# A fused attention and feed-forward layer on one core: even parts of the relative values, the output mask at the end of the step, and a low part on GpSimd

## The reference

```python
xn  = layernorm(x)
q,k,v = projections of xn with biases                     # [B,H,S,8]
idx = clip(r[None,:] - r[:,None], -128, 128) + 128
scores = (einsum('bhqd,bhkd->bhqk', q, k) + einsum('bhqd,qkd->bhqk', q, rel_k[idx])) / sqrt(8)
w   = softmax(scores)
att = einsum('bhqk,bhkd->bhqd', w, v) + einsum('bhqk,qkd->bhqd', w, rel_v[idx])
ffn = relu(xn @ ternary(W1).T + b1) @ ternary(W2).T + b2
out = x + att @ Wo.T + bo + ffn
```

## Time and profile before

| | us |
|---|---|
| median of 3 runs | 612.52 (611.48 to 612.66) |
| the profiled execution | 610.89 |
| its span in the profile | 609.1 |
| busy in the span: PE, DVE, ACT, POOL | 533.7, 508.8, 466.0, 149.5 |
| end of the first stage (barrier on SP's queue) | 108.8 |
| transposes of step 0, of step 127 | 112.6, 567.4 |
| table work of DVE in the second chunk (L563 to L581) | 42.5 to 45.5 |

### The profile page before, as it was taken

The page is one execution under the profiler, slowest core; times in us unless marked ns, Lnnn a source line. Parts: engine busy times, 40 slices in busy tenths (PEclk is TensorE's granted clock), DMA queues, the critical chain, the costliest instruction groups (busy, mean ns, idle before and its releaser), DMA issues.

```text
span 609.1 us, 25643 instructions
## 1 busy us (share of the span) xinstructions
PE 533.7 (88%) x10578; PEld 489.7 (80%) x10578; DVE 508.8 (84%) x1353; ACT 466.0 (77%) x993; POOL 149.5 (25%) x170
## 2 busy tenths in 40 slices
PE   0777796689999999999999999999999999999996
PEld 0354464578989898898989898999898989898896
DVE  6798967699888989888888888888888888989734
ACT  1686885589887978898889788878887898879511
POOL 4345554032222213131313131313122222210000
PEclk9997999799999999999999999989999999999778
DMA  8312565911000010101010101010100001000243
GB/s 184 125 45 77 129 111 133 161 27 29 12 20 15 17 23 8 27 7 28 4 29 4 30 3 30 2 30 5 26 11 22 13 19 18 15 3 4 64 116 104
DMA packets 75835, 26.34 MB, mean 43 GB/s; under 512 B 55008, under 2 KB 72904, under 8 KB 75592
## 3 DMA queue, kind: packets, MB, share of 16 engines
q1 hardware_dynamic: 74832, 24.19, 17.9%
q10 hardware_dynamic: 888, 0.53, 0.3%
HBM read 13.16 MB, written 8.40 MB: 35 GB/s over the span
## 4 chain that ended last, share of the span: by engine, by line
PE 51%; DVE 15%; issue 14%; ACT 1%; DVEq 0%; ACTq 0%
PE ps_r L878 11%; PE ps_r L880 10%; PE ps_s L950 8%; PE ps_o L848 6%; DVE obd L1143 5%; PE ps_t L938 5%; PE ps_o L852 4%; PE ps_o L850 4%; DVE mcol L1180 3%; DVE big L1113 2%; DVE mx L1109 2%; PE ps_s L902 1%; PE ps_y L862 1%; PE ps_t L927 1%; PE ps_o L927 1%
## 5 line engine op out<-in xcount | busy, mean ns | idle before, releaser
L756 POOL COPY by_q_room<-qrel 96x256 uint32<-96x256 uint32 x120 | 98.3, 821 | 340.8 <-PE ps_t L938 293.9
L1113 DVE TENSOR_TENSOR big<-p,big 128x512 f16<-128x512 f32 x256 | 172.1, 673 | 0.1
L1027 ACT ACTIVATE big<-p 128x512 f16<-128x512 f32 x256 | 161.5, 632 | 6.1 <-PE ps_r L880 6.1
L878 PE MATMUL ps_r<-gwin,big 128*128 128x17 f16 x1024 | 133.3, 207 | 0.0
L880 PE MATMUL ps_r<-gwin,big 128*128 128x9 f16 x1024 | 132.6, 203 | 0.0
L1180 DVE TENSOR_REDUCE mcol<-ps_t 128x4 bf16<-128x512 bf16 x128 | 88.2, 689 | 53.0 <-PE ps_t L938 53.0
L880 PEld LDWEIGHTS ps_r<-gwin,big 128*128 128x128 f16 x1024 | 128.2, 164 | 0.0
L878 PEld LDWEIGHTS ps_r<-gwin,big 128*128 128x128 f16 x1024 | 125.9, 162 | 0.0
L1007 ACT ACTIVATE p<-ps_s 128x512 f32<-128x512 f32 x128 | 77.8, 607 | 46.0 <-PE ps_s L950 44.0
L848 PE MATMUL ps_o<-v_sb,big 128*128 128x33 f16 x1024 | 90.6, 178 | 21.5 <-DVE obd L1143 7.8
L848 PEld LDWEIGHTS ps_o<-v_sb,big 128*128 128x128 f16 x1024 | 80.9, 96 | 33.0 <-issue 31.7
(11 more groups left out here) (110 smaller groups left out, 873.7 us busy)
## 6 DMA issues: line engine op xcount, KB each, us to landing
kst<-big SPq DMA_DIRECT2D x48, 64.0 KB, 2.0
qrel<-qr_dram SPq DMA_DIRECT2D x192, 16.0 KB
qbd<-q_dram SPq DMA_DIRECT2D x192, 16.0 KB
q_dram<-by_q_room SPq DMA_DIRECT2D x8, 256.0 KB, 3.1
y_dram<-big SPq DMA_DIRECT2D x4, 512.0 KB, 4.4
qr_dram<-big SPq DMA_DIRECT2D x4, 512.0 KB, 8.3
big<-y_dram SPq DMA_DIRECT2D x4, 512.0 KB, 6.9
out<-big SPq DMA_DIRECT2D x4, 512.0 KB, 3.2
```

The lines of the kernel that those rows point to most:

```text
L878: nc.tensor.matmul(r_ps[:, q % QH, :], hi, win, start=(q % QH == 0 and kh == 0), stop=False, skip_group_check=True)
L1027: nc.scalar.activation(probs[:, k // 8, 0, kh, k % 8, :], p32[:, k % 2, kh, :], ACT.Copy).then_inc((hi0_ready, hi_ready)[kh], 1)
L1113: nc.vector.tensor_tensor(probs[:, k // 8, 1, kh, k % 8, :], p32[:, k % 2, kh, :], probs[:, k // 8, 0, kh, k % 8, :], ALU.subtract).then_i ...
```

## The change

Seven edits. In the main stage: (1) `REL_PARTS` is eight parts of 4 queries, from step 9 + 8 bg on, so every step has one; the sums follow (at 13 + 8 bg + 4 half). (2) The mask of the outputs moves from the start of the next step to the end of its own, after the head mask. (3) The low part of the second 128 keys is made on POOL, with a semaphore of its own. (4) POOL's half copies are dealt to other steps (`HALVES`), at most two in a step, the last in step 1 of the group itself. In the first stage: (5) `residues` moves from ACT to POOL, between its other work; (6) the low parts of hidden blocks 2 and 3 move from POOL to DVE, ahead of the copies of V; (7) the clearing of `qbd` moves ahead of the first deviations.

```diff
-REL_PARTS = (4, 4, 4, 4, 5, 5, 6)
+REL_PARTS = (4,) * 8
...
# first stage, ACT
-                wait(act, hlo_ready, c * FT + f - 1)
+                wait(act, hlo_ready[1 - f // 2], FT // 2 * (c + f // 2 - 1) + f % 2 + 1)
...
-                    residues(q_hi, 0, i, p).then_inc(qhi_ready, 1)
...
-                    residues(q_lo, 1, i, p).then_inc(qlo_ready, 1)
# first stage, POOL
+            def residues(part, s, i, p):
+                pool.wait_ge((nat_hi_ready, nat_lo_ready)[s], 2 * i + p + 1)
+                own = part.rearrange("p (n j x q y) -> p n j x q y", n=NQB, j=J, x=B // 2, y=2)[:, :, :, 2 * i + p, :, :]
+                for b in range(2):
+                    ins = nc.gpsimd.tensor_copy(own[:, :, :, :, b],
+                                                q_nat[:, i % 2, s, :, 2 * p + b, :].rearrange("p n (q j) -> p n j q", j=J))
...
+            nc.gpsimd.memset(v["qbd"]...).then_inc(zero_q, 1)
             inverse_deviation(0, 0)
             inverse_deviation(1, 1)
-            nc.gpsimd.memset(v["qbd"]...).then_inc(zero_q, 1)
...
                     if not last:
                         inverse_deviation(2 * i + p + 2, p)
-                    for f in range(FT):
-                        hidden_low(2 * i + p, f)
+                    residues(q_hi, 0, i, p).then_inc(qhi_ready, 1)
+                    hidden_low(2 * i + p, 0)
+                    residues(q_lo, 1, i, p).then_inc(qlo_ready, 1)
+                    hidden_low(2 * i + p, 1)
# first stage, DVE, after normalize and before the copies of V
+                    for f in range(FT // 2, FT):
+                        dve.wait_ge(hhi_ready, c * FT + f + 1)
+                        nc.vector.tensor_tensor(hid[:, 1, f, :], hf[:, f % 2, :], hid[:, 0, f, :],
+                                                ALU.subtract).then_inc(hlo_ready[1], 1)
# main stage, POOL
-    BY_Q = ((), (), (), (0,), (1,), (2,), (), (3,))
+    HALVES = (((2, 1), (3, 0)), ((3, 1),), (), (), ((0, 0),), ((0, 1),), ((1, 0), (1, 1)), ((2, 0),))
...
+            def low_part(qb, k):
+                pool.wait_ge(hi_ready, UNITS * qb + k + 1)
+                nc.gpsimd.tensor_tensor(probs[:, k // 8, 1, 1, k % 8, :], p32[:, k % 2, 1, :],
+                                        probs[:, k // 8, 0, 1, k % 8, :], ALU.subtract).then_inc(lo1_ready, 1)
...
+                    su = qb * BG + k // 8 + (k % 8 >= 4)
+                    for x, half in HALVES[k % 8] if 0 < su < NQB * BG else ():
                         pool.wait_ge(qrel_in, (su + 1) * (16 * NDMA))
                         pool.wait_ge(scores_ready, 8 * (su - 1) + 2 * x + 2)
                         pool.wait_ge(maxT_ready, n + 1)
-                        half_pair(x, 0)
-                        pool.wait_ge(half_copied, n + 2)
-                        pool.wait_ge(scores_ready, n + 2)
-                        half_pair(x, 1)
+                        half_pair(x, half)
+                    if unit(qb, k - 1):
+                        if n + 1 < ALL:
+                            pool.wait_ge(half_copied, n + 2)
+                            pool.wait_ge(scores_ready, n + 2)
+                        low_part(*unit(qb, k - 1))
# main stage, PE
-                pe.wait_ge(lo_ready, KH * (n + 1))
+                pe.wait_ge(lo0_ready, n + 1)
+                pe.wait_ge(lo1_ready, n + 1)
...
+                if first == 0:
+                    pe.wait_ge(lo0_ready, UNITS * qb + 8 * bg + 8)
+                    pe.wait_ge(lo1_ready, UNITS * qb + 8 * bg + 8)
...
-                        part = k + UNITS * back - (10 + 8 * bg)
+                        part = k + UNITS * back - (9 + 8 * bg)
# main stage, DVE
-                    if unit(qb, k - 4):
-                        mask_outputs(*unit(qb, k - 4))
...
-                        low_part(*unit(qb, k - 1), 0)
+                        low_part(*unit(qb, k - 1))
...
-                    if unit(qb, k - 1):
-                        low_part(*unit(qb, k - 1), 1)
...
+                    if unit(qb, k - 3):
+                        mask_outputs(*unit(qb, k - 3))
```

More of the change, by code:

```diff
@@ L381, in hidden @@
                                      bias=bcol[:, 2 + f:3 + f]).then_inc(hhi_ready, 1)
[L383 to L389, removed]
             copy_xT(0, 0)
@@ L401, in body @@
                         act.wait_ge(nat_out[i % 2], 32)
+                        act.wait_ge(qhi_ready, 2 * i - 2)
+                        act.wait_ge(qlo_ready, 2 * i - 2)
                     nc.scalar.activation(q_nat[:, i % 2, 0, :, 2 * p:2 * p + 2, :], natural(ps_o[:, :]),
                                          ACT.Identity, bias=bcol[:, 0:1]).then_inc(nat_hi_ready, 1)
-                    act.wait_ge(nat_hi_ready, c + 1)
-                    residues(q_hi, 0, i, p).then_inc(qhi_ready, 1)
                     if not (last and p == 1):
@@ L431, in inverse_deviation @@
                 nc.gpsimd.tensor_tensor(rstd[:, p, :], vare[:, p, :], neghalf[:, :], ALU.pow).then_inc(rstd_ready, 1)
+            def residues(part, s, i, p):
[4 more added lines that the diff above has]
+                                                q_nat[:, i % 2, s, :, 2 * p + b, :].rearrange("p n (q j) -> p n j q", j=J))
+                return ins
             def hidden_low(c, f):
                 pool.wait_ge(hhi_ready, c * FT + f + 1)
-                nc.gpsimd.tensor_tensor(hid[:, 1, f, :], hf[:, f % 2, :], hid[:, 0, f, :], ALU.subtract).then_inc(hlo_ready, 1)
+                nc.gpsimd.tensor_tensor(hid[:, 1, f, :], hf[:, f % 2, :], hid[:, 0, f, :], ALU.subtract).then_inc(hlo_ready[0], 1)
+            nc.gpsimd.memset(v["qbd"][:, :, :, :, :].rearrange("p s g h c -> p (s g h c)").bitcast(F32), 0.0).then_inc(zero_q, 1)
             inverse_deviation(0, 0)
             inverse_deviation(1, 1)
-            nc.gpsimd.memset(v["qbd"][:, :, :, :, :].rearrange("p s g h c -> p (s g h c)").bitcast(F32), 0.0).then_inc(zero_q, 1)
             def body(i, last):
@@ L630, in down @@
                 for f in range(FT):
-                    pe.wait_ge(hlo_ready, c * FT + f + 1)
+                    pe.wait_ge(hlo_ready[f // 2], FT // 2 * c + f % 2 + 1)
                     for t in range(CH):
@@ L721, in build_main @@
         shifted0, shifted, exp0_ready, hi0_ready = sem("shifted0"), sem("shifted"), sem("exp0_ready"), sem("hi0_ready")
-        hi_ready, lo_ready = sem("hi_ready"), sem("lo_ready")
+        hi_ready, lo0_ready, lo1_ready = sem("hi_ready"), sem("lo0_ready"), sem("lo1_ready")
         rsum_ready, gwin_ready, ewin_ready = sem("rsum_ready"), sem("gwin_ready"), sem("ewin_ready")
@@ L760, in body @@
                     n = UNITS * qb + k
-                    for x in BY_Q[k % 8] if not (last and k >= 8) else ():
-                        su = qb * BG + k // 8 + 1
+                    su = qb * BG + k // 8 + (k % 8 >= 4)
+                    for x, half in HALVES[k % 8] if 0 < su < NQB * BG else ():
                         pool.wait_ge(qrel_in, (su + 1) * (16 * NDMA))
@@ L1004, in exponentials @@
                 act.wait_ge(shifted0, n + 1)
-                wait(act, lo_ready, KH * (n - 1))
+                wait(act, lo0_ready, n - 1)
                 nc.scalar.activation(p32[:, k % 2, 0, :], ps_s[:, k % 2, 0, :], ACT.Exp, scale=SCALE).then_inc(exp0_ready, 1)
                 act.wait_ge(shifted, n + 1)
+                wait(act, lo1_ready, n - 1)
                 nc.scalar.activation(p32[:, k % 2, 1, :], ps_s[:, k % 2, 1, :], ACT.Exp, scale=SCALE).then_inc(exp_ready, 1)
@@ L1109, in maximum, with low_part @@
                 nc.vector.tensor_tensor(mx[:, :], s0[:, :], ps_s[:, k % 2, 1, :], ALU.max).then_inc(max_ready, 1)
[L1111 to L1114, removed]
+            def low_part(qb, k):
+                dve.wait_ge(hi0_ready, UNITS * qb + k + 1)
+                nc.vector.tensor_tensor(probs[:, k // 8, 1, 0, k % 8, :], p32[:, k % 2, 0, :],
+                                        probs[:, k // 8, 0, 0, k % 8, :], ALU.subtract).then_inc(lo0_ready, 1)
             def low_outputs(qb, k):
@@ L1168, in relative_of @@
                     for half in range(2):
-                        at = 14 + 8 * bg + 3 * half
+                        at = 13 + 8 * bg + 4 * half
                         if k == at % UNITS and (at < UNITS or unit(qb, -1)):
@@ L1244, in _ @@
             outputs(UNITS - 3)
-            low_part(NQB - 1, UNITS - 1, 0)
-            low_part(NQB - 1, UNITS - 1, 1)
+            low_part(NQB - 1, UNITS - 1)
             low_outputs(NQB - 1, UNITS - 3)
```

5 lines of the change are left out of this document (2 added, 3 removed).

## The result

The changed kernel takes 565.12 us (564.79 to 565.31, four runs) against 612.12 (611.48 to 612.66, four runs beside it): ratio 0.9232, 95% interval 0.9216 to 0.9248, 47 us less. The forecast was 573.5 with a range of 560 to 597. The direction and the place of the gain were right.

The account below looks back on a forecast made before the run. Neither PE nor DVE alone bounds it: pv hangs on transposes, reduce and mask. Span 609.1 + 5 (first stage) - 1.3 (early steps) - 42.7 (117 steps) = 570.1, so 573.5 us for the median; range 560 to 597.

Parts of the forecast that it names:

- The chain through the mask: Main loop: pv hangs on transposes, reduce, mask; the mask at the step's end saves 0.29 us per step.
- The term for the uneven steps: Main loop: eight parts of 4 queries remove PE's 0.49 us wait for the maximum in one step of eight.
- DVE's margin: Main loop: the maximum ends 0.7 us before its transposes, 0.3 with sums; the mask ends as the next reduce is due.
- The port: Main loop: POOL and DVE instructions with SBUF operands exclude each other; head mask waits for POOL's low part, ending at 3.4.
- Rival S: Each step: POOL and DVE exclude each other for every instruction; 4.33 us a step, 124 over the forecast, 697; chance 0.07.
- a pushed L1113: Main loop: a POOL copy delays DVE's low part by 0.15, up to 0.8 in two steps of eight; nothing set.
- the low part's leaving: Main loop: the second low part goes from DVE to POOL, taking 0.58 us a step off DVE.
- The ten early steps: Ten steps before relative products: DVE loses some seven low parts and PE's waits before pv go; 1.3 us saved.
- The first stage: Projections and feed-forward: clearing qbd earlier -3.4, loop through POOL +7.7, last chunks +2.4, gap at the end -2.0; +5.
- the price of a copy: First stage: a POOL copy of 256 f16 elements taken at 0.61 us, making a chunk 11.75 us, +7.7 over five.
- Rival D: First stage costs nothing: a copy costs 0.33 and the loop doesn't close, only -3.4 is left; 565; chance 0.12.
- the 8 us that would follow: First stage: by the skill's page a copy costs about half of 0.61, making the total some 8 us less.

Follow-up runs that it names:

- the last pair: Changed kernel with GpSimd's hidden low parts 0 and 1 ahead of residues and gwin pieces one step earlier: 559.86 us; same with second low part on DVE: 561.67.

## Why the prediction was right, step by step

**The chain through the mask: right.** 0.29 us a step and 0.49 of eight were forecast. Undoing the mask alone costs 0.29 a step. `pv` stands 1.15 after the transposes (forecast 1.17), and the step takes 3.247 (forecast 3.27). The term for the uneven steps is a little small: over eight steps, even parts alone save 0.73 in the windows and taking them back costs 0.58.

**DVE's margin: right in size, wrong in what it would look like.** The reduce starts 0.42 after the transposes, and the chain of low part, maximum, head mask and mask ends at 308.23, when the next reduce is due: "it just fits". But the forecast looked for that margin as idle time before the reduce, above 53 us. It is in the duration of L1154. Other signs missed as well: the head mask takes 0.51 in the median and not 0.7, and the first scores start at 109.4 and not at 114 to 115.

**The port: right for POOL's low part, wrong in its use.** The head mask waits for it in nearly every step, as predicted, and the output mask with its operand from PSUM doesn't. Rival S, an exclusion for every instruction, is refuted: maximum L1130 at 306.39 runs its 0.68 us across the start of POOL's low part. The Trainium skill (SBUF — State Buffer, SBUF: two separate sides) says that a VectorE operation with two SBUF inputs and a GpSimd operation that reads SBUF hold the shared port in turn, each for its whole instruction. The rows agree: 0.17 becomes 0.74 beside the low part, 0.66 becomes 1.11 beside a copy. What the forecast missed is that the copies' place in the step matters more than the low part's engine: it priced a pushed L1113 at nothing and the low part's leaving as a part of the gain. The runs give some 9 to 11 us to the first and 1 to 3 to the second.

**The ten early steps: wrong.** -1.3 was forecast, +0.6 measured, and these are two things. First, the gain didn't come: steps 4 to 9 take 18.7 us in both kernels. The chain named in the forecast (POOL's low part, head mask, mask, next reduce) is what decides. In most of these steps DVE is busy without a break, and PE waits 0.35 to 0.77 us for its maximum. DVE's order takes 2.95 us in four of the six before, and 2.8 to 3.2 in the changed kernel, where the head mask is held (0.32 to 0.53 us instead of 0.17) and the output mask stands right behind it and reads its result. With the low part back on DVE the head mask isn't held, and the order takes 3.1 to 3.2 in most of them. PE timeline of the changed kernel:

```profile
132.81 0.40 PE L957 MATMUL ps_t<-identb,mx 128*128 128x128 bf16 x4 [0.77 <-DVE mx L1130]
```

Second, the +0.6 lies in one step, the second of the ten, and in the granted clock. That step before and after, as windows (columns as in the earlier trace rows; the clock is the third number from the end):

```profile
115.76:118.35 2.59, 1.91 (x37) 1.61 (x36) 2.02 (x4) 2.59 (x6) 0.00 (x0) 1.00 0.44 104
115.29:118.46 3.17, 3.00 (x37) 2.81 (x36) 1.98 (x3) 2.72 (x6) 0.36 (x1) 0.58 0.44 103
```

The step's 37 matrix instructions take PE 3.00 us at a clock of 0.58 and 1.91 at 1.00; in the step before, the clock is at its lower level (0.50 and 0.51) in both kernels. In the kernel of the last pair with the low part on GpSimd, the clock of this step is 0.90, and it takes 2.59. So the forecast's account of the engines has no part in the +0.6. Why the clock rises a step later in most kernels with the new main stage wasn't tried.

**The first stage: the step that failed is the price of a copy.** The forecast had the loop right (variance, inverse deviation, two copies, low part, two copies, low part, hidden 3, DVE's low part, next variance) and priced a copy at 0.61, the row of a copy with as many elements of another type. The copies' own row in the changed kernel:

```profile
L428 POOL COPY big<-by_q_room x32: 465/474/507, 22.3 to 97.5; 128x256 f16<-128x256 f16 x32
```

And two of them take 0.78 from their start to that of the low part behind them (46.78 to 47.56): 0.39 each. The chunk is then 11.75 - 4 x 0.22 = 10.87; measured 10.76. In the terms of the sum: the five chunks cost +2.5 (56.77 against 54.23 between the third and the last inverse deviation, here and in the earlier trace rows) instead of +7.7, the last two chunks and the end -0.5 instead of +0.4, and the clearing of `qbd` gives -2.4 (21.31 against 23.70) instead of -3.4.

```profile
21.31 1.01 POOL L421 TENSOR_TENSOR rstd<-vare,neghalf 128x4 f32<-128x4 f32 x1 [11.96 <-DVE vare L476]
...
78.08 1.01 POOL L421 TENSOR_TENSOR rstd<-vare,neghalf 128x4 f32<-128x4 f32 x1 [5.94 <-DVE vare L476]
```

DVE's timelines, before and after, show why the clearing gives less. The eight normalisations are 3.0 shorter, not 3.4, and without the hold DVE arrives at a load that is late:

```profile
8.23 5.32 DVE L482 TENSOR_SCALAR big<-big,obd,rstd 128x128 f32<-128x128 f32 x8
```

```profile
8.14 2.36 DVE L483 TENSOR_SCALAR big<-big,obd,rstd 128x128 f32<-128x128 f32 x8
11.08 0.29 DVE L494 TENSOR_TENSOR xr<-xr 128x128 f32<-128x128 f32 x1 [0.57 <-DMA xr<-in_b]
```

Together -0.4. Rival D (a copy at 0.33, 565 us) gave the time that was measured, but not for its reason: the loop does close, as the order of GpSimd's work shows. The Trainium skill (GPSIMD Engine Reference, 4.1 Engine selection) says that GpSimd is about 2x slower for operations with two inputs and roughly at line rate with one; it compares GpSimd with VectorE. The forecast took from it half the price of a copy, named the 8 us that would follow, and set them aside. The rows of the changed kernel bear this out in direction and not in size: 256 elements in 0.39 is 1.5 ns each, against 1.10 / 512 = 2.1 for the low part (46.78 to 47.56 and 47.56 to 48.66), and half of 0.61 would have been 0.31. The uint32 copy, with 0.62 for 256 elements, stays at 2.4.

**Sum.** -0.4 + 0.6 - 45.5 - 1.0 = -46.3 of span, forecast -39. The first stage holds 5.4 of the 7.3 us between them. The 117 steps gave 2.8 more than forecast and the tail 1.0; the early steps gave 1.9 less and so hid a part of the error.

## What to carry to other kernels

Find the operation that frees a buffer for the bottleneck engine and count what stands ahead of it in its engine's order; here its place was worth 22 to 35 us, depending on what else had been changed, at an equal cost of the operation itself. When an instruction is much longer than its size explains, look which instruction of the neighbour engine ends with it: that time is a wait, and neither idle time nor busy shares show it. Before work goes to a second engine for relief, price where in the step that engine's other work falls: here that was worth some 9 to 11 us, and the relief 1 to 3. And move an operation with an eye on who then comes second: the mask's new place made DVE wait for GpSimd's copies, where GpSimd had waited for DVE.

## What the runs showed of the hardware that was not expected

- A GpSimd copy of 128x256 f16 takes 0.39 us from start to start (0.474 in the records); one of 96x256 uint32 takes 0.62. Elements alone don't give the price. Whether the type or the layout makes it wasn't tried.
- Of the 3.0 us that the clearing of `qbd` had held DVE's normalisations (5.32 less 2.36), 2.4 came through: behind them DVE met a load that was late by 0.57, and that can't be seen while the hold is there.
- Work that fits in a long step can bound a short one: the same DVE order leaves PE no wait for the maximum in steps of 3.25 us and one of 0.35 to 0.77 us in early steps of 2.8 to 3.2.
- The granted clock can rise a step later in one kernel than in another at the same work: 0.58 against 1.00 in the second step, which is the 0.6 us that the early steps lost.
